# Code search of a four-stage image block: the fourth block search moved to the third step, fine searches one or two units later

## What is computed

```python
d = jnp.sum(z_flat ** 2, axis=1, keepdims=True) + jnp.sum(codebook ** 2, axis=1) - 2.0 * jnp.matmul(z_flat, codebook.T)
idx = jnp.argmin(d, axis=1)
z_q = codebook[idx].reshape(B, H, W, C)
...
x = x + _L1_conv_ref(_gn(x), L1_conv_codebook)
```

## Time and profile before

| | |
|---|---|
| median of 3 runs | 1626.82 us (1622.72 to 1631.12) |
| span of the profiled execution | 1625.7 us |
| search, chunks 0 to 8 | about 297 to 797 us of the span |
| busy in the whole span | PE 74%, DVE 83%, ACT 27%, POOL 63% |

### The profile page before, as it was taken

The page is one execution under the profiler, slowest core; times in us unless marked ns, Lnnn a source line. Parts: engine busy times, 40 slices in busy tenths (PEclk is TensorE's granted clock), DMA queues, the critical chain, the costliest instruction groups (busy, mean ns, idle before and its releaser), DMA issues. The chain is left out here.

```text
span 1625.7 us, 19842 instructions
## 1 busy us (share of the span) xinstructions
PE 1203.1 (74%) x6050; PEld 749.5 (46%) x6094; DVE 1347.6 (83%) x1880; ACT 432.4 (27%) x1363; POOL 1027.7 (63%) x983
## 2 busy tenths in 40 slices
PE   5898999799888998888856676576655566545565
PEld 2454555344444444444445454454444344434444
DVE  5578898799999999898858989997787777888776
ACT  1241000124443343252456231221212211111111
POOL 6169798614443343136777677777777777777773
PEclk9889999799999999999978897787777867766777
DMA  5041000011211111054466797787877878777774
GB/s 170 14 154 55 1 0 0 15 48 44 59 55 44 34 46 55 5 172 133 147 219 190 224 289 208 210 270 228 249 208 229 251 229 250 209 234 210 210 209 145
DMA packets 111102, 232.65 MB, mean 143 GB/s; under 512 B 14676, under 2 KB 60500, under 8 KB 110748
## 3 DMA queue, kind: packets, MB, share of 16 engines
q0 software_dynamic: 58176, 191.30, 39.7%
q1 hardware_dynamic: 52828, 40.17, 7.8%
HBM read 205.15 MB, written 26.26 MB: 142 GB/s over the span
## 5 line engine op out<-in xcount | busy, mean ns | idle before, releaser
L2147 POOL DMA_INDIRECT code_region<-corners,lead_region x252 | 242.0, 960 | 77.9 <-issue 75.2
L1927 DVE SCALAR_TENSOR_TENSOR max_region<-score,nc,max_region 128x512 f32<-128x512 f32 x324 | 231.2, 742 | 33.3 <-PE score L1481 31.2
L772 POOL TENSOR_TENSOR prod_acc<-prod_acc,prod_pool 128x768 f32<-128x768 f32 (+8 forms) x118 | 172.0, 1457 | 61.5 <-DVE prod_pool L747 52.6
L2147 POOL DMA_INDIRECT early_region<-corners,lead_region x136 | 129.1, 949 | 41.3 <-issue 40.5
L1518 PE MATMUL score<-ident,code_region 128*128 128x128 f32 x540 | 95.7, 338 | 78.5 <-DVE code_region L1984 74.0
L2147 POOL DMA_INDIRECT max_region<-corners,lead_region x130 | 123.6, 951 | 41.3 <-issue 38.7
L2147 POOL DMA_INDIRECT late_region<-corners,lead_region x126 | 119.4, 948 | 43.2 <-issue 37.5
L1927 DVE SCALAR_TENSOR_TENSOR max_region<-lead_score,nc,max_region 128x512 f32<-128x512 f32 x180 | 132.5, 743 | 8.9 <-PE lead_score L1481 8.2
L1518 PEld LDWEIGHTS score<-ident,code_region 128*128 128x128 f32 x540 | 78.0, 175 | 94.9 <-DVE code_region L1984 87.8
L2062 POOL DMA_INDIRECT late_region<-code_rows,block_id x35 | 35.9, 1026 | 135.3 <-DVE block_id L1765 99.0
L1980 DVE TENSOR_TENSOR lead_score<-lead_score,code_region 128x768 f32<-128x768 f32 x78 | 75.4, 966 | 38.9 <-DMA code_region<-corners,lead_region 35.8
(11 more groups left out here) (298 smaller groups left out, 3089.0 us busy)
## 6 DMA issues: line engine op xcount, KB each, us to landing
corners<-lead_region SPq DMA_DIRECT2D x72, 192.0 KB
corners<-lead_region SPq DMA_DIRECT2D x8, 576.0 KB
code_rows<-codes_n SPq DMA_DIRECT2D x8, 516.0 KB, 3.8
codes_t<-in_codes_t SPq DMA_DIRECT2D x8, 512.0 KB, 3.7
codes_n<-in_codes SPq DMA_DIRECT2D x8, 512.0 KB, 4.1
code_region<-corners,lead_region POOLq DMA_INDIRECT x252, 3.7
x<-in_x SPq DMA_DIRECT2D x2, 1152.0 KB, 6.4
out<-x SPq DMA_DIRECT2D x4, 576.0 KB, 3.1
```

The costliest lines, as they stand in the source:

```text
L772: pool.tensor_tensor(to, to, v, ALU.add).then_inc(pooled, 1)
L1927: dve.scalar_tensor_tensor(r, score[SLOT[k]], nc2[:, m:m + 1], r, ALU.add, ALU.max).then_inc(dve_took, 1)
L2147: pool.indirect_dma_start(quad(T, k), None, table[j].rearrange("n s c -> n (s c)"), bass.IndirectOffsetOnAxis(index[j % B][:, at:at + 1], 0))\
```

## The change

The dictionary is replaced by a function that gives the places for each chunk, `select` looks them up, and it is now also asked in the loop over units 0 and 1, which DVE itself does not take: parts placed at k = 0 or 1 stand ahead of unit 2. A mechanism for chunks whose search runs on into the next chunk (`SPILLED`) is added, but its range is empty, so those branches issue nothing. `subtract_z` moves from behind `lead` of unit (3, 15) to ahead of it. PE's `turn_zq` gets a wait on the subtraction of the chunk before, on which `turn_z` has waited earlier in the same chunk.

```diff
+    SPILLED = range(0)
+    ZQ_TURN_AT = 3
...
             def turn_zq(n):
 
                 pe.wait_ge(zq_in, 16 * PXT * n)
+                pe.wait_ge(delta_ready, n)
...
-            parts = {(0, 12): (find, 0), (0, 14): (place_block, 0), (1, 2): (find, 1), (1, 4): (place_block, 1),
-                     (1, 6): (find, 2), (1, 8): (place_block, 2), (1, 10): (find, 3), (1, 12): (place_block, 3),
...
+            def selection(n):
+
+                if n in SPILLED:
...
+                elif n == L0:
+                    finds, fines, subtract = ((0, 12), (1, 2), (2, 0), (2, 10)), ((2, 4), (2, 13), (3, 4), (3, 9)), (3, 15)
+                else:
+                    finds, fines, subtract = ((0, 12), (1, 2), (1, 8), (2, 1)), ((2, 4), (2, 9), (3, 3), (3, 8)), (3, 15)
+                at = {(s, k + i): (part, n, u) for u, (s, k) in enumerate(finds) for i, part in ((0, find), (1, place_block))}
+                at.update({(s, k + i): (part, n, u) for u, (s, k) in enumerate(fines)
+                           for i, part in ((0, fine_find), (1, fine_place))})
+                at[subtract] = subtract_z, n, None
+                return at
...
+                for k in range(BY_ACT):
+                    select(n, s, k)
                 for k in range(BY_ACT, NPR):
...
-                    if n and (s, k) in parts:
-                        part, u = parts[s, k]
-                        part(n, u)
+                    select(n, s, k)
                     lead(n, s, k)
-                if n and s == STEPS - 1:
-                    subtract_z(n)
```

More of the change, by code:

```diff
@@ L1485, in step @@
                         turn_z(n)
+                    if k == ZQ_TURN_AT and n - 1 in SPILLED and s == 1:
+                        turn_zq(n - 1)
                     lead(n, s, k)
-                if n and s == STEPS - 1:
+                if n and s == STEPS - 1 and n not in SPILLED:
                     turn_zq(n)
@@ L1653, in step @@
                         .then_inc(act_took, 1)
+                if n - 1 in SPILLED and s == 0:
+                    sum_products(n - 1, 3)
                 if n and s >= 2:
-                    sum_products(n, 2 * (s - 2) + 1)
+                    sum_products(n, s - 1 if n in SPILLED else 2 * (s - 2) + 1)
                 lead(n, s, False)
@@ L1661, in step @@
                     keep_z(n)
-                if n and s in (1, 2):
+                if n and (s == 1 or s == 2 and n not in SPILLED):
                     sum_products(n, 2 * (s - 1))
@@ L2096, in add, with spilled_step @@
                 pool.tensor_tensor(x_flat[:, at], x_flat[:, at], delta, ALU.add).then_inc(x_added, 1)
+            def spilled_step(n, s):
+                if s == 1:
+                    gather(n, 0)
+                    gather(n, 1)
+                    multiply(n, 0)
+                    if n - 1 in SPILLED:
+                        add(n - 1)
+                    multiply(n, 1)
+                if s == 2:
+                    gather(n, 2)
+                    fetch(n, 0)
+                    fetch(n, 1)
+                    multiply(n, 2)
+                if s == STEPS - 1:
+                    gather(n, 3)
+                    fetch(n, 2)
+                    multiply(n, 3)
             def step(n, s):
@@ L2100, in step @@
                     return
+                if n - 1 in SPILLED and s == 0:
+                    fetch(n - 1, 3)
+                if n in SPILLED:
+                    return spilled_step(n, s)
                 last = n == NPX - 1
```

19 lines of the change are left out of this document (13 added, 6 removed).

## The result

The changed kernel takes 1631.79 us (median of 16 runs, 1629.15 to 1637.11), the kernel before 1626.81 us in the runs beside it. The ratio is 1.0029, with a 95% interval from 1.0019 to 1.0039: slower by 4.7 us (3.1 to 6.3). The profiled execution has a span of 1630.1 us, 4.4 us more than before.

The account below looks back on a forecast made before the run. DVE's queue sets the pace from the first step's unit 12 into the third step, PE behind that. Terms -0.1 + 1.4 + 0.9 + 1.3 = +3.5 us on the median 1626.82 gave 1630.3 us, range 1622 to 1637.

Parts of the forecast that it names:

- chunks 1 to 5: Ordinary chunks: PE gains 0.59 us each, the later fourth fetch takes back all but 0.09 us; -0.1 us taken in sum.
- chunks 6 and 7: Chunk 6 +1.4 us, mainly the index ahead of `pooled`; chunk 7 +0.9 us, PE waiting for the later last fetch.
- last fetch of chunk 8: Chunk 8's last index comes 1.31 us later and POOL's queue behind the search follows: +1.3 us.
- The walk: Ordinary chunks, through the five PE/DVE buffers: of 2.4 us moved, 0.59 us are left at PE's unit 8, third step.
- the start of the transposition: End of ordinary chunks: fetch issued at 442.53, lands at 445.13, PE ready at 444.56; all but 0.09 us taken back.
- The term of 1.2 us for the index: Chunk 6: the second tile's index ahead of the chain to `pooled` makes taps and all units behind 1.2 us later.
- The range's upper end for the low clock (+3 us): Chunk 6's upper end: the low clock that follows the longer wait lasts longer, +3 us instead of +1.4 us.
- the same walk through the buffers: Chunk 8: PE's unit 8 of the third step comes at the time it has now, so no gain.
- A: Landings met or fine search not last: ordinary chunks keep 0.59 us each, chunk 7 costs nothing; 1626.6 us, chance 0.20.
- B: DVE idle in the third step: each of eight chunks gains up to 2.35 us; 1609.3 us, half 1618; chance 0.06.
- C: All fourth fetches take 3.4 to 3.6 us to land: +9.2 us, 1636.0 us; chance 0.10.
- D: PE's clock falls once in each of eight chunks after longer waits: +9.6 + 3.5, 1640 us; chance 0.04.

Follow-up runs that it names:

- weigh later: The changed kernel with chunk 8's chain of gather weights on DVE one unit later, behind unit (2, 15) instead of (2, 14); ratio 1.0031 to before.
- index behind norm: The changed kernel with chunk 6's second block-search index back behind unit (1, 4), so behind the normalisation chain and `pooled`; ratio 1.0016 to before.
- weigh earlier: The changed kernel with chunk 8's chain of gather weights on DVE three units earlier, behind (2, 11) instead of (2, 14); ratio 1.0025 to before.

## Why the prediction was right, and where not

The forecast was 1630.3 us, the measured median 1631.8 us, no change by the 0.5% bound and slower by 0.3%. By its terms:

| term | forecast | measured | from |
|---|---|---|---|
| chunks 1 to 5 | -0.1 | -0.9 | 5 x 0.19, periods 51.09 and 50.90 |
| chunks 6 and 7 | +1.4 + 0.9 | +1.6 | 146.0 less 144.4, slow stretches of equal length |
| last fetch of chunk 8 | +1.3 | +2.8 | 54.9 less 52.1 |
| POOL's queue behind it | 0 | +0.8 | first gather to last fetch 44.2 and 45.0, mean of profiles |
| sum | +3.5 | +4.3 | ratio: 4.7 (3.1 to 6.3) |

The total is near in part by luck: the ordinary chunks and chunks 6 and 7 came out 0.8 and 0.7 us below their terms, the two rows behind them 1.5 and 0.8 us above.

**Ordinary chunks.** The walk was right in size and place: waits at units 8 and 15 of the second step, for DVE at unit 8 of the third, gain 0.60 us. The wait at unit 8 of the second step was smaller than forecast, 1.54 us and not 2.06. By the forecast's own rows it should have read 1.91 us (0.69, and 412.41 to 413.63); 0.16 us had been waited before (404.99), and some 0.2 us stay unexplained. The step that failed is the start of the transposition: I let some 2.75 us pass from issue to transposition, and it is 2.61 us, since load and matmul start together when the row is waited for. The forecast chose 2.6 us from chunk 2's row and bounded it by 3.4 us for chunk 1. In the changed kernel chunk 1's transposition comes 2.75 and 2.91 us behind the issue (two profiles); with only the fine searches late and with weigh later it comes at 3.38 and 3.34 us, and PE waits 0.98 and 0.94 us. So late landings do occur there, and that neither profile of the changed kernel has one may be chance.

**Chunk 6.** The term of 1.2 us for the index is what L224 shows (1.19 us), in every profile, though the sign that I named, a wait 1.2 us longer, shows by 0.55 us at L224 and by 0.65 us at the wait before it. The range's upper end for the low clock (+3 us) is what the first trace after seemed to show, but before has that stretch too, in one profile of three. Averaged over all profiles of either kernel chunks 6 and 7 cost 2.8 us instead of 1.6; how often each stretch comes isn't known from so few.

**Chunk 7** was priced at the long landing of 3.6 us and the short one of 2.5 us, in the middle. From the fetch at 737.13 to the transposition 2.76 us pass, and PE waits 0.28 us for it, the lower end. In the changed kernel's second profile it is 3.16 us and 1.06 us, above the middle that I took; yet the way from chunk 5's transposition is only 0.3 us longer there (145.85 and 146.11 us).

**Chunk 8.** The step that failed is "the same walk through the buffers gives PE's unit 8 of the third step the time that it has now". It moved DVE's chain of weights by some 2.4 us against POOL and never asked what POOL runs there. Of the +2.8 us the fine search's delay is 1.3 to 1.7 us (1.3 expected), and the other 1.1 to 1.5 us belong to the moved block search and that meeting together; the meeting alone was not measured. Such a meeting stood in chunk 7 of the trace that I had read (725.52, above). The queue behind added 0.8 us that I hadn't counted, and its cause isn't shown: from the first gather to the last fetch the kernels with a late last fetch take 43.7 to 45.8 us, the others 43.6 to 44.5 us. POOL's first L2195 comes 498.3 us behind DVE's first unit in both profiles of the changed kernel, the first L2147 at 494.1 us in the mean of before: 4.1 us later, where I had named 3.5.

**Rivals.** A (the balance pays) is false for the changed kernel and true once the fine searches are back: 50.49 us is its 50.5 us. B is out: in the third step unit 8 waits 0.91 us for DVE. C is out for the changed kernel: its landings were 2.5 to 2.7 us in the first profile, and in the second only chunks 1 and 7 were later (2.91 and 3.16 us to the transposition). D is out for the ordinary chunks (granted clock 1.00 from 395 to 600 us in all kernels); with weigh earlier, weigh later and index behind norm it did fall in chunk 8.

## What to carry over

Moving one engine's work in its queue changes what it meets on the other engines: before a move, list what POOL multiplies at the new time of every small DVE instruction that works in SBUF alone, not of the moved one only, and look in the trace of before for a small one that ends just behind a POOL instruction. A gain on PE of 0.6 us is only kept if the step that comes last behind it moves with it; here half of the change earned 0.60 us per chunk and the other half gave back 0.4. And a difference of 1.6 us between two traces at one place may be the clock of that execution: profile the kernel before a second time before a reason is looked for.

## What the runs showed of the hardware

- A DVE TENSOR_TENSOR of 0.2 us (128x54, all in SBUF) that meets a POOL TENSOR_TENSOR of 2.19 us ends 0.06 to 0.08 us behind it, in chunk 8 six times in six. In chunk 7 a TENSOR_SCALAR of the same size does the same in before (2.20 us, ending 0.05 us behind). The longest TENSOR_TENSOR of the chain took 2.22 us (index behind norm, chunk 7).
- PE at the 1.2 GHz level stays there for 3.4 or 6.8 us in sum behind the same wait of 3.15 us, in executions of the same kernel, and the longer one goes with 1.6 us more time.
- The time of the first 300 us, before the search, varies more than the change is worth: the first unit is taken by DVE at 298.1 to 303.7 us in the profiles, in before alone at 300.7, 302.3 and 300.6 us. Starts of a stage were therefore compared as differences within one trace.
